# Rotation of q and k in a transformer block: halves swapped by transfers and summed on GpSimd, with all instruction orders laid anew

## The reference, cut to what matters

```python
xn = layernorm(x)
q, k, v = xn @ wq, xn @ wk, xn @ wv            # 16 x 8 heads x 512 x 128
q, k = rope(q), rope(k)
s = q @ k.T / 128 - 1e30 * (i < j)
attn = (softmax(s) @ v) @ wo
h = s0 * concat(xn, -xn) @ sign(k0); h = relu(h) * 2      # 1024 wide
h = s1 * h @ sign(k1);               h = relu(h) * 2      # 1024 wide
return x + attn + s2 * h @ sign(k2)

def rope(x):                                   # even, odd: the two halves of the 128
    return concat(even * cos - odd * sin, even * sin + odd * cos)
```

## Time and profile before

| | before |
|---|---|
| runs, median (lowest to highest) | 1717.77 us (1715.64 to 1720.3), 3 runs |
| the profiled execution, its own time | 1720.49 us |
| its span in the trace | 1718.7 us |
| mean granted TensorE clock | 0.996 |
| busy PE, DVE, ACT, POOL | 99%, 84%, 86%, 56% of the span |
| DMA | 125.13 MB, mean 73 GB/s |

### The profile page before, as it was taken

How to read it: one execution, slowest core, us unless ns; L and a number is a source line. 1 busy time by engine, 2 the same in 40 slices (tenths; PEclk the granted TensorE clock), 3 DMA queues, 4 the chain that set the end, 5 groups by cost and what they waited for, 6 DMA issues and landing times.

```text
span 1718.7 us, 34113 instructions
## 1 busy us (share of the span) xinstructions
PE 1701.7 (99%) x12600; PEld 1205.8 (70%) x12600; DVE 1450.2 (84%) x3503; ACT 1479.2 (86%) x3250; POOL 967.1 (56%) x767
## 2 busy tenths in 40 slices
PE   8999999999999999999999999999999999999999
PEld 5566767777677676776767677776776767667677
DVE  7998798887988889888887888879888898887975
ACT  6898898888988889888898888888888898888984
POOL 6764647556564565645556465564655656456522
PEclk8999999999999999999999999999999999999999
DMA  5232433424333333432434334333332434333333
GB/s 178 44 59 50 106 64 75 84 53 90 62 74 68 72 72 62 84 66 64 77 63 90 62 71 78 62 75 72 76 73 59 84 62 84 59 71 71 62 71 63
DMA packets 416405, 125.13 MB, mean 73 GB/s; under 512 B 396272, under 2 KB 415216, under 8 KB 416240
## 3 DMA queue, kind: packets, MB, share of 16 engines
q1 hardware_dynamic: 416240, 122.97, 36.1%
HBM read 14.94 MB, written 8.39 MB: 14 GB/s over the span
## 4 chain that ended last, share of the span: by engine, by line
PE 96%; DVE 2%; ACT 1%; DMA 1%; SPq 0%; issue 0%; DVEq 0%
PE bank L275 36%; PE bank L803 21%; PE bank L771 12%; PE bank L754 12%; PE bank L792 8%; PE bank L814 6%; DMA ph<-in_wv 1%; PE bank L782 0%; DVE bank L660 0%; ACT bank L498 0%; ACT ph L502 0%; DVE hb L624 0%; DVE rt L675 0%; DVE bank L632 0%; DVE tb L636 0%
## 5 line engine op out<-in xcount | busy, mean ns | idle before, releaser
L406 POOL TENSOR_TENSOR qk<-tb,qk 128x512 f16<-128x512 f32 x256 | 295.8, 1161 | 327.4 <-ACT qk L475 327.3
L403 POOL TENSOR_TENSOR tb<-tb,sin 128x512 f32<-128x512 f32 x256 | 325.3, 1274 | 271.5 <-ACT tb L472 269.6
L803 PE MATMUL bank<-hb,wa 128*128 128x256 f16 x3360 | 382.2, 273 | 0.0
L803 PEld LDWEIGHTS bank<-hb,wa 128*128 128x128 fp8e5 x3360 | 327.5, 98 | 38.9
L498 ACT ACTIVATE bank<-bank,nm,sc 128x512 f32<-128x512 f32 (+3 forms) x512 | 301.4, 589 | 2.9
L670 DVE SCALAR_TENSOR_TENSOR ph<-bank,rk,ph 128x256 f16<-128x256 f32 (+3 forms) x512 | 251.5, 544 | 27.6 <-ACT ph L502 26.9
L660 DVE CUSTOM_DVE_ANT_0 bank<-bank,mask 128x128 f32<-128x128 f32 (+3 forms) x512 | 237.9, 517 | 15.0 <-PE bank L754 14.7
L502 ACT ACTIVATE ph<-bank,rk 128x512 f16<-128x512 f32 (+3 forms) x512 | 230.6, 537 | 10.2 <-DVE rk L667 10.0
L754 PE MATMUL bank<-qk 128*128 128x512 f16 (+3 forms) x1536 | 230.1, 299 | 3.1 <-DVE tb L636 1.6
L471 ACT ACTIVATE tb<-bank 64x512 f32<-64x512 f32 x256 | 151.9, 593 | 89.0 <-PE bank L275 81.1
L771 PE MATMUL bank<-pt,v 128*128 128x512 f16 (+3 forms) x1536 | 227.1, 299 | 0.6 <-DVE hb L683 0.4
(11 more groups left out here) (140 smaller groups left out, 2622.0 us busy)
## 6 DMA issues: line engine op xcount, KB each, us to landing
out<-xnat SPq DMA_DIRECT2D x32, 256.0 KB, 2.1
xnat<-in_x SPq DMA_DIRECT2D x15, 512.0 KB, 3.9
pt<-ph SPq DMA_TRANSPOSE x128, 4.9
o<-in_k SPq DMA_DIRECT2D x1, 1024.0 KB, 7.9
v<-in_wq SPq DMA_DIRECT2D x1, 1024.0 KB, 9.9
v<-in_wk SPq DMA_DIRECT2D x1, 1024.0 KB, 11.6
ph<-in_wv SPq DMA_DIRECT2D x1, 1024.0 KB, 14.1
o<-in_wo SPq DMA_DIRECT2D x1, 1024.0 KB, 10.8
```

The costliest lines, as they stand in the source:

```text
L403: pool.tensor_tensor(tb, tb, SIN[:], ALU.mult).then_inc(s_crossed, 1)
L406: pool.tensor_tensor(QK[:, g % 2, 2 * w + 1, :], TB[:, (2 * g + w) % TRING, :], QK[:, g % 2, 2 * w, :], ALU.subtract).then_inc(s_qk_lo, 1)
L803: mm = pe.matmul(ps[:, 256 * u:256 * u + 256], WA[:, w, k, (2 * j + u) * 128:(2 * j + u) * 128 + 128], HB[:, h, s, k, :], start=first and ...
```

## The change

Each q or k tile is copied once from PSUM to SBUF by ACT (TA, a ring of 2). SP swaps its halves by two plain transfers of 64 partitions x 2 KB into TB (now a ring of 3). DVE writes `bank * COS` into a third ring TS (3 tiles) and no longer back to PSUM, which frees the bank. POOL multiplies TB by SIN as before and now also makes the sum TS + TB, in SBUF; `rotate` on DVE is gone. A tile has a number n in order of use, and a has it in order of copying.

```diff
-TRING = 4
+TA_RING, TB_RING, TS_RING = 2, 3, 3
+        def exchange(sp, a, n):
+            ta, tb = TA[:, a % TA_RING, :], TB[:, n % TB_RING, :]
+            sp.dma_start(tb[0:64], ta[64:128]).then_inc(s_turned[n % TB_RING], 16)
+            sp.dma_start(tb[64:128], ta[0:64]).then_inc(s_turned[n % TB_RING], 16)
+        def rotate(pool, n):
+            ts = TS[:, n % TS_RING, :]
+            pool.tensor_tensor(ts, ts, TB[:, n % TB_RING, :], ALU.add).then_inc(s_rot, 1)
-        def swap(act, g, w, ps):
...
+        def copy_tile(act, a, ps):
+            act.activation(TA[:, a % TA_RING, :], ps[:, :], ACT.Copy).then_inc(s_tile, 1)
-        def straight(dve, ps):
-            dve.tensor_tensor(ps[:, :], ps[:, :], COS[:], ALU.mult).then_inc(s_straight, 1)
-
-        def rotate(dve, g, w, ps):
...
+        def straight(dve, n, ps):
+            dve.tensor_tensor(TS[:, n % TS_RING, :], ps[:, :], COS[:], ALU.mult).then_inc(s_straight, 1)
```

All five lists are new, and so are the banks; no batch is a loop body any more, though batches 3 to 14 repeat one order of `qk`, `scores` and `values`. TensorE's list has the same calls, each as often as before. Two stretches of the new lists matter to the prediction. The loads at the start, and DVE's first calls:

```diff
         def sync_program(sp):
+            load_x_rest(sp)
             load_x_first(sp)
-            load_x_rest(sp)
+            load_k(sp, 1)
+            load_k(sp, 0)
             load_scales(sp)
-            load_k(sp, 0)
-            load_k(sp, 1)
             load_w(sp, "q")
+            load_sin(sp)
             load_w(sp, "k")
             load_cos(sp)
-            load_sin(sp)
-            load_k(sp, 2)
             load_w(sp, "v")
-            load_x(sp, 1)
             sp.wait_ge(s_k0, 4)
             load_w(sp, "o")
+            load_k(sp, 2)
+            load_x(sp, 1)
```

More of the change, by code:

```diff
@@ L1225, in gpsimd_program @@
[L1225 to L1227 removed]
+            qk_lo(pool, 11, 1, 23)
+            pool.wait_ge(s_turned[1], 288)
+            crossed(pool, 25)
+            pool.wait_ge(s_crossed, 26)
+            pool.wait_ge(s_straight, 26)
+            rotate(pool, 25)
+            pool.wait_ge(s_turned[2], 288)
+            crossed(pool, 26)
+            pool.wait_ge(s_crossed, 27)
+            pool.wait_ge(s_straight, 27)
+            rotate(pool, 26)
@@ new lines, in gpsimd_program @@
+            crossed(pool, 76)
+            pool.wait_ge(s_qk_hi, 75)
+            qk_lo(pool, 37, 0, 74)
+            pool.wait_ge(s_crossed, 77)
+            pool.wait_ge(s_straight, 77)
+            rotate(pool, 76)
+            rotate(pool, 75)
+            rstd(pool, 5)
+            pool.wait_ge(s_qk_hi, 76)
+            qk_lo(pool, 36, 1, 75)
+            pool.wait_ge(s_turned[2], 832)
+            crossed(pool, 77)
+            pool.wait_ge(s_rstd, 6)
+            normalise(pool, 5)
+            pool.wait_ge(s_crossed, 78)
@@ new lines, in gpsimd_program @@
+            rotate(pool, 92)
+            rotate(pool, 91)
+            rstd(pool, 6)
+            pool.wait_ge(s_qk_hi, 92)
+            qk_lo(pool, 44, 1, 91)
+            pool.wait_ge(s_turned[0], 1024)
+            crossed(pool, 93)
+            pool.wait_ge(s_rstd, 7)
+            normalise(pool, 6)
+            pool.wait_ge(s_crossed, 94)
+            pool.wait_ge(s_straight, 94)
+            rotate(pool, 93)
+            pool.wait_ge(s_qk_hi, 93)
+            qk_lo(pool, 46, 0, 92)
+            pool.wait_ge(s_xp_hi, 6)
@@ new lines, in gpsimd_program @@
+            rotate(pool, 106)
+            pool.wait_ge(s_qk_hi, 106)
+            qk_lo(pool, 53, 1, 105)
+            pool.wait_ge(s_turned[2], 1152)
+            crossed(pool, 107)
+            pool.wait_ge(s_turned[0], 1184)
+            crossed(pool, 108)
+            pool.wait_ge(s_qk_hi, 107)
+            qk_lo(pool, 53, 0, 106)
+            pool.wait_ge(s_crossed, 109)
+            pool.wait_ge(s_straight, 109)
+            rotate(pool, 108)
+            rotate(pool, 107)
+            rstd(pool, 7)
@@ new lines, in gpsimd_program @@
+            pool.wait_ge(s_qk_hi, 124)
+            qk_lo(pool, 60, 1, 123)
+            pool.wait_ge(s_turned[2], 1344)
+            crossed(pool, 125)
+            pool.wait_ge(s_rstd, 9)
+            normalise(pool, 8)
+            pool.wait_ge(s_crossed, 126)
+            rotate(pool, 125)
+            pool.wait_ge(s_qk_hi, 125)
+            qk_lo(pool, 62, 0, 124)
+            pool.wait_ge(s_xp_hi, 8)
+            xp_lo(pool, 8)
+            pool.wait_ge(s_xp, 8)
+            x_sums(pool, 8)
@@ new lines, in gpsimd_program @@
+            pool.wait_ge(s_turned[0], 1536)
+            crossed(pool, 141)
+            pool.wait_ge(s_rstd, 10)
+            normalise(pool, 9)
+            pool.wait_ge(s_crossed, 142)
+            pool.wait_ge(s_straight, 142)
+            rotate(pool, 141)
+            pool.wait_ge(s_qk_hi, 141)
+            qk_lo(pool, 70, 0, 140)
+            pool.wait_ge(s_xp_hi, 9)
+            xp_lo(pool, 9)
+            pool.wait_ge(s_xp, 9)
+            x_sums(pool, 9)
+            pool.wait_ge(s_qk_hi, 142)
@@ new lines, in gpsimd_program @@
+            pool.wait_ge(s_qk_hi, 188)
+            qk_lo(pool, 92, 1, 187)
+            pool.wait_ge(s_turned[0], 2048)
+            crossed(pool, 189)
+            pool.wait_ge(s_rstd, 13)
+            normalise(pool, 12)
+            pool.wait_ge(s_crossed, 190)
+            rotate(pool, 189)
+            pool.wait_ge(s_qk_hi, 189)
+            qk_lo(pool, 94, 0, 188)
+            pool.wait_ge(s_xp_hi, 12)
+            xp_lo(pool, 12)
+            pool.wait_ge(s_xp, 12)
+            x_sums(pool, 12)
@@ new lines, in gpsimd_program @@
+            pool.wait_ge(s_rstd, 15)
+            normalise(pool, 14)
+            pool.wait_ge(s_crossed, 222)
+            rotate(pool, 221)
+            pool.wait_ge(s_qk_hi, 221)
+            qk_lo(pool, 110, 0, 220)
+            pool.wait_ge(s_xp_hi, 14)
+            xp_lo(pool, 14)
+            pool.wait_ge(s_xp, 14)
+            x_sums(pool, 14)
+            pool.wait_ge(s_qk_hi, 222)
+            qk_lo(pool, 111, 1, 221)
+            pool.wait_ge(s_turned[0], 2400)
+            crossed(pool, 222)
```

17554 lines of the change are left out of this document (13274 added, 4280 removed), and 16 rows, old and new, of the table ROTATION.

## The result

| kernel | median | runs | profiled span |
|---|---|---|---|
| before | 1717.77 us | 1715.64 to 1720.3 | 1718.7 us |
| changed | 1792.06 us | 1792.01 to 1793.13 | 1791.3 us |

The ratio is 1.0434, with a 95% interval of 1.041 to 1.0457. The change costs 74 us; I had forecast 1724, with 1742 as the upper end. The direction was the likeliest one, the size was not in the range.

The account below looks back on a forecast made before the run. PE was taken to bound the kernel, at 104.9 us a batch. The profiled 1720.5 + 3.9 (tightest place) + 2 (start) + 0 (batches 0 to 2, end) gave 1726.4, less 2.7 to the median 1723.7 us; range 1709 to 1742.

Parts of the forecast that it names:

- What bounds the kernel: In the loop of some thirteen batches PE never idles: a floor of 104.9 us a batch.
- The sum of what could be won: Outside the loop: PE's idle time and slow clock, some 11.6 us back at most.
- Part 1: ACT loses 147 us and DVE 174 us of work, worth 0 us in the thirteen batches beside PE.
- Part 2: POOL gains 256 sums of 1.27 us, 326 us, reaching 1293 us or 75% of the span; fits on the average.
- Part 3: Each exchange takes 2.6 us from SP's being free to both halves landed, bounds 2.1 and about 6.5.
- Part 4: Around head 8b+4 of each batch: margin 0.9 us, PE waits 0.3 us, 13 times, +3.9 us, bounds 0 and +20.
- Part 5: At the start, k0 and scales land later and DVE normalises 4.7 us later: +2 us, bounds -3 and +5.
- Part 6: Batches 0 to 2: 0 us, bounds -5 and +8; the end: 0 us, bounds 0 and +2.6.
- D: Rival: each exchange's halves go one after the other, 4.7 us in place of 2.6: 1746 us, chance 0.09.
- A: Rival: the whole kernel as the terms were summed, 1719 to 1732 us, chance 0.42.
- B: Rival: no wait in the thirteen batches and a start that comes out even, 1717 to 1719 us, chance 0.22.
- C: Rival: the start gains, its 2.5 us wait and slow clock go, lighter ACT and DVE help: 1710.8 us, chance 0.27.

Follow-up runs that it names:

- both costs out: The changed kernel with one transfer for each pair (halves not exchanged) and GpSimd's sum on 8 of 512 columns: 1739.85 us, ratio 1.0126.
- The thin sum: The changed kernel with GpSimd's sum made for 8 of the 512 columns only, all waits and lists kept: 1749.32 us, ratio 1.0184.

## Why the prediction was wrong, point by point

- **What bounds the kernel** held in the loop. The floor of 104.9 us a batch is the floor of the changed lists too: with both costs out, late batches take 104.87. "The change can only hold it or break it" came true in the second way. The sum of what could be won was too small: before, the clock was also below 1.00 from 10 to 20 us (0.85) and from 30 to 60 (0.94).
- **Part 1** held: ACT fell by 167.5 us (forecast 147), DVE by 150.5 (174), worth nothing. The runs with the swap back on ACT suggest that the new order even lives on ACT's room.
- **Part 2** held in its size (1.275 us a sum; POOL 1278.7 us, forecast 1293). "On the average it fits" was true and decided nothing.
- **Part 3** was mis-sized: 2.6 us from a free SP to both halves landed. The second issue takes 0.60 us behind 0.51 for the first (medians), and the landing is 2.4, not 2.1. `crossed` started 2.88 us after the first issue at the earliest and 3.31 in the median where POOL had been idle. So the path was 0.3 to 0.7 us longer than my sum, against a margin of 0.9 that I had worked out myself. The run with one transfer prices 0.53 us of it at 39 us.
- **Part 4** is the step that failed. "What waits behind POOL then is `normalise` and both sums of the next x, which come later and have more room" is wrong: the runs with `tp_lo` moved show that a delay there holds SP's transpose, and behind it probability tiles and exchanges, at 33 of 48 us. I had followed POOL's list against PE's, one place long, and not POOL's against SP's. So I took 0.3 us a batch at head 8b+4; the trace has 0.13 there, 1.2 at head 8b+6, and some 3.3 in all: 33.9 us over batches 4 to 14. My upper bound of 20 for the whole term was too low, because I bounded one place and took the rest for covered. One reading was wrong too: exchange 140 waits for sum 137, not 138 (the ring has three tiles), and in each of batches 3 to 14 it was issued before sum 138 had ended. The named place had more room than I gave it.
- **Part 5** was mis-sized: +2 taken, +4.7 measured (42.05 against 37.33 us), near the bound of +5. DVE's L586 begins at 12.60 against 12.2 by my sum, but `layer0` starts at 20.32 and not at 18.2, and its 32 matmuls do not run without a break: the last eight start at 27.66. With the old order of loads the 4.7 are gone.
- **Part 6** failed in size: 0 with +8 as its bound, and it is +20.2 in batches 0 to 2; at the end, 0 with +2.6 as its bound, and it is +9.2. I wrote that POOL would be over 100% from 60 to 80 us and still took zero. The thin sum and the single transfer leave +9.4 of it together and +4.6 at the end; what the rest hangs on was not tried.
- **The rivals.** D came nearest in time (1746), but not by its mechanism. A second half that waited for the first would have cost its whole landing; it cost its issue, 0.53 us. "The halves go one after the other" is not what the trace shows: each lands 2.4 us after its own issue. And its tile 140 does not wait for sum 138. The rule of the Trainium skill (DMA: Bandwidth & Descriptors, "Rules for kernel authors") gave the right advice all the same, one transfer over 128 partitions: here it is worth 39 us, though it can't swap halves. It gives no time for the pair; the 4.7 us of D were my reading of it. A would have needed the path to be as short as summed; B and C are out.

What is settled: the sum and the second transfer together make some 52 of the 74 us, and they overlap. That both are one cost, a path some 0.6 us too long for the room in interlocked lists, is the reading that fits; path and SP's time were not parted. The other 20 us in the trace with both removed: 5.7 ahead of the first q product, 9.4 in batches 0 to 2, 4.6 at the end. The old order of loads gave 8 us back by itself; whether that adds to the 52 was not run, and the rest stays open.

## What to carry to other kernels

When a change lengthens a step's path under hand-laid lists, add up the path against the room at every place where it passes a list, and follow each list to the ones that it releases: here POOL's `tp_lo` was a gate for SP's transposes, and these for PE. A load of 71% says nothing when the margin is 0.9 us; count every issue and a hand-over for each hop, and if the margin is then below its uncertainty, price it as broken in every repetition. And take the zero out of a sum where you have just written "over 100%".

## What the runs showed of the hardware

- One more issue of a transfer costs SP 0.5 to 0.6 us, however small the transfer: with 64 KB each, 2.0 us to landing in place of 2.4 at 128 KB. Four transfers of 64 KB gave `crossed` its start 0.7 to 1.0 us later than two of 128 KB.
- SP is held by the issue of a DMA transpose for 1.75 to 4.12 us, as the rows above show; a plain transfer behind it in the list can't start in that time.
- The same sum of two float32 tiles in SBUF takes 1.275 us on GpSimd, as the product with a constant does (1.274). On DVE it takes 0.68 us, but where it began while GpSimd ran it often ended only 0.55 us after GpSimd's end (87 of 256, 1.58 us in the mean, up to 2.63).
